# A fused attention, MLP and mixture-of-experts kernel: scores read by half, mask table on GpSimd

## The reference

```python
scores = jnp.einsum('bqhd,bkhd->bhqk', q, k)              # q = layernorm(x), k = v = context, 16 heads of 16
scores = jnp.where(mask == 0, jnp.float32(-1e+20), scores)
attn = jax.nn.softmax(scores / jnp.float32(E ** 0.5), axis=3)
out = jnp.einsum('bhqk,bkhd->bqhd', attn, v).reshape(b, l, e) @ W_out.T + b_out
```

## Time and profile before

| | us |
|---|---|
| median of 3 runs | 1400.29 (1398.33 to 1403.54) |
| the profiled execution, its own time | 1391.09 |
| its span, first to last instruction | 1389.3 |
| attention, first instruction to the next stage's first | 393.8 |
| busy in the span: PE, VectorE, ScalarE, GpSimd | 1225.5, 908.9, 628.3, 576.5 |
| mean granted clock of TensorE | 0.966 |

### The profile page before, as it was taken

One profiled execution on the slowest core, in us unless ns is written; L12 is line 12 of the kernel. 1 busy time (PEld: TensorE's weight loads), 2 busy tenths in 40 slices (PEclk: granted clock), 3 DMA queues, 4 the chain that ended last, 5 costly groups with the idle time before them and its releaser, 6 DMA issues. The chain is left out here.

```text
span 1389.3 us, 29923 instructions
## 1 busy us (share of the span) xinstructions
PE 1225.5 (88%) x10852; PEld 940.3 (68%) x10852; DVE 908.9 (65%) x2674; ACT 628.3 (45%) x1081; POOL 576.5 (41%) x604
## 2 busy tenths in 40 slices
PE   3699999999847798997579999897999999999996
PEld 1355555555423366886467988776999998999995
DVE  7898898898869773225456577444666566665663
ACT  2577777777555571334216633222333333333331
POOL 6899999999900000003200004661333333333333
PEclk9999999999959999999898999999999999999999
DMA  6344344245220001110329205326888877888781
GB/s 225 98 147 138 95 147 141 94 144 190 100 91 0 1 1 46 45 30 1 100 84 255 58 1 183 112 89 214 262 249 250 262 242 248 250 250 257 244 244 65
DMA packets 104193, 196.40 MB, mean 141 GB/s; under 512 B 15632, under 2 KB 86928, under 8 KB 91552
## 3 DMA queue, kind: packets, MB, share of 16 engines
q1 hardware_dynamic: 89792, 178.21, 39.9%
q0 software_dynamic: 14304, 16.93, 5.7%
HBM read 144.70 MB, written 52.23 MB: 142 GB/s over the span
## 5 line engine op out<-in xcount | busy, mean ns | idle before, releaser
L1992 PE MATMUL banks<-moe_w,moe_hT 128*128 128x256 f16 x2640 | 300.6, 273 | 7.2 <-issue 7.1
L1992 PEld LDWEIGHTS banks<-moe_w,moe_hT 128*128 128x128 f16 x2640 | 258.8, 98 | 40.5 <-issue 9.9
L1903 ACT ACTIVATE moe_hf<-banks,moe_b 128x256 f32<-128x256 f32 x440 | 184.9, 472 | 182.7 <-PE banks L1979 148.7
L1847 POOL DMA_INDIRECT out_x<-moe_y,slot_owner x78 | 122.0, 1565 | 285.4 <-DVE moe_y L2225 255.9
L1979 PE MATMUL banks<-moe_rT,moe_w 128*128 128x256 f16 x1872 | 211.8, 273 | 0.0
L745 DVE CUSTOM_DVE_ANT_0 masked<-banks,mask_bias 128x256 f32<-128x256 f32 x512 | 185.8, 418 | 22.6 <-PE banks L515 21.9
L1979 PEld LDWEIGHTS banks<-moe_rT,moe_w 128*128 128x128 f16 x1872 | 183.8, 98 | 21.3
L405 ACT ACTIVATE probsT<-banks 128x1024 f32<-128x1024 f32 x128 | 131.3, 1026 | 64.2 <-PE banks L541 64.1
L2112 DVE TENSOR_TENSOR moe_hT<-moe_hf,moe_hT 128x512 f16<-128x512 f32 x220 | 153.6, 698 | 7.6
L2110 DVE CAST moe_hT<-moe_hf 128x512 f16<-128x512 f32 x220 | 95.2, 433 | 64.1 <-ACT moe_hf L1903 43.9
L1833 POOL DMA_INDIRECT slots_x<-moe_xn,pos x64 | 65.0, 1015 | 153.4 <-DVE pos L2176 123.3
(11 more groups left out here) (323 smaller groups left out, 2006.7 us busy)
## 6 DMA issues: line engine op xcount, KB each, us to landing
moe_w<-moe_halves SPq DMA_DIRECT2D x80, 1024.0 KB, 5.0
moe_halves<-w_cut SPq DMA_DIRECT2D x18, 1024.0 KB, 8.6
slots_x<-empty_row SPq DMA_DIRECT2D x1, 10140.0 KB, 48.8
moe_rows<-slots_x SPq DMA_DIRECT2D x39, 260.0 KB, 5.8
w_in<-in_L_ffn_Wfc SPq DMA_DIRECT2D x8, 1024.0 KB, 6.3
w_in<-in_L_ffn_Wproj SPq DMA_DIRECT2D x8, 1024.0 KB, 6.5
moe_b<-in_L_ffn_bproj SPq DMA_DIRECT2D x39, 128.0 KB
ctx_rows<-in_ctx SPq DMA_DIRECT2D x16, 256.0 KB, 2.8
```

The source lines that it names most:

```text
L1847: pool.indirect_dma_start(out=out_rows, out_offset=bass.IndirectOffsetOnAxis(ap=owner[:, s, t:t + 1], axis=0), in_=y[s % 2][:, t, :], in_o ...
L1903: ins = act.activation(hf[p][:, j, :], src, ACT.Gelu_apprx_tanh, bias=b1[buffer][:, j:j + 1], scale=1.0 / WSCALE)
L1992: ins = pe.matmul(OUT[p][:, t * D:(t + 1) * D], hT[p][:, x, j, t * P:(t + 1) * P], w2[buffer][:, w, j, :], start=(j == 0 and (w, x) == PAR ...
```

## The change

The changed kernel differs in five things.

1. Scores by half. `scores` now issues one matmul: head j of the pair, rows t. PE makes the two scores matmuls of one head and the two transposed ones of the other head (`both_scores(B, hp, 0)`), then a part of the side work, then the other halves (`both_scores(B, hp, 1)`) and the mask. `take_max` reads one half and counts in `s_red` for each, so a half of `psum_s` is free as soon as it has been read.
2. The side work has another order. `fill` 0 goes through `psum_o` and is copied by VectorE, 1 and 2 by ScalarE, 3 by VectorE; the two calls of `project` and `add` are one each; ScalarE's copies stand ahead of the exponent of their head pair.
3. GpSimd makes the mask table (`set_all`), one batch ahead, at the end of its phase behind `split_k`; for batches 0 and 1 before the loop and at the end of its first phase. VectorE waits for `s_ma`.
4. The cutting of the experts' weights (`load_half`, `store_half`, `cut_piece`, now functions of their own with buffers that live through three stages): 9 halves beside attention, two pieces in each phase; 2 beside the MLP, two pieces ahead of its first reduction over partitions, six behind it; 7 in the autocorrelation, ahead of its bias adds. The stores are waited for at the end of the autocorrelation.
5. `mixT` of the autocorrelation lies in the memory of `zf`, and `see_weights` stands behind the first half of the head pair.

```diff
+def load_half(sp, d, w, n):
+    src = expert_half(d, n)
+    if n >= 2:
+        sp.wait_ge(w["cut"], 3 * PIECES * (n - 1))
+    sp.dma_start(w["rows"][n % 2][:].rearrange("p (k f) -> p k f", k=src.shape[1]), src).then_inc(w["in"][n % 2], 16)
+def store_half(sp, w, halves_dram, n):
+    sp.wait_ge(w["cut"], 3 * PIECES * (n + 1))
...
+def cut_piece(pool, w, q):
+    n, i = q // PIECES, q % PIECES
...
+    if i == 0:
+        pool.wait_ge(w["in"][n % 2], 16 * (n // 2 + 1))
+    if i == 0 and n >= 2:
+        pool.wait_ge(w["stored"][n % 2], 16 * (n // 2))
+    pool.tensor_scalar(rows[:, cols], rows[:, cols], WSCALE, None, ALU.mult).then_inc(w["cut"], 1)
...
             for b in range(NB):
                 if b >= 2:
                     load_ctx(b)
                     load_mask(b)
-                load_half(b)
-                if b >= 2:
-                    store_half(b - 2)
+                if b < 2:
+                    load_half(sp, d, w, b)
+                elif b % 2 and (b + 1) // 2 < CUT_BESIDE_ATTENTION:
+                    load_half(sp, d, w, (b + 1) // 2)
+                    store_half(sp, w, halves_dram, (b + 1) // 2 - 2)
...
+            def set_all(b):
+                s = b % 2
+                pool.wait_ge(s_mask[s], 16 * (b // 2 + 1))
+                if b >= 2:
+                    pool.wait_ge(s_mb, b - 1)
+                pool.tensor_scalar(mask_all[s][:], mask_int[s][:], 0, MASKED, ALU.is_equal, ALU.mult).then_inc(s_ma, 1)
+
+            split_k(0)
+            set_all(0)
             for B in PHASES:
-                if real(B + 2):
-                    split_k(B + 2)
                 if B >= -1:
-                    cut(B + 1, 0, PIECES // 2)
+                    cut_piece(pool, g.cut, 2 * (B + 1))
                 if real(B + 2):
                     split_q(B + 2)
...
                 if real(B + 2):
                     add_bias(B + 2)
                 if B >= -1:
-                    cut(B + 1, PIECES // 2, PIECES)
+                    cut_piece(pool, g.cut, 2 * (B + 1) + 1)
+                if real(B + 3):
+                    split_k(B + 3)
+                    set_all(B + 3)
...
+            def both_scores(B, hp, j):
+                for i in range(NQ):
+                    if real(B + 1):
+                        scores(B + 1, hp, j, i)
+                    if real(B):
+                        scoresT(B, hp, 1 - j, i)
...
             for B in PHASES:
                 for hp in range(HP):
+                    both_scores(B, hp, 0)
+                    if hp == 0 and real(B + 2):
...
+                        fill(B + 2, 0)
+                    if hp == 1 and real(B - 1):
...
+                        weigh(B - 1, 3)
+                    if hp == 2 and real(B + 1):
...
                         mask_back(B + 1)
...
+                    if hp == 6 and real(B - 1):
...
+                        project(B - 1)
...
+                    both_scores(B, hp, 1)
+                    if real(B):
+                        scoresT_mask(B, hp)
+                    if hp == 0 and real(B):
+                        pe.wait_ge(s_r, 2 * B + 1)
+                        max_back(B, 1)
...
+            see_mask(0)
+            norm_end(0)
             for B in PHASES:
                 for hp in range(HP):
                     if hp == 0 and real(B):
                         split_max(B, 1)
...
+                    if real(B + 1):
+                        take_max(B + 1, hp, 0)
+                    if hp == 0 and real(B + 2):
+                        fill(B + 2, 0)
+                    if hp == 1 and real(B + 2):
+                        set_live(B + 2)
...
+                    if hp == 5 and real(B + 3) and B == -2:
+                        see_mask(B + 3)
+                    if hp == 0 and real(B + 2) and B >= 0:
+                        see_mask(B + 2)
+                    if hp == 6 and real(B + 2):
+                        fill(B + 2, 3)
                     if hp == 6 and real(B - 1):
-                        add(B - 1, 0)
...
+                        add(B - 1)
+                    if B == NB and hp == 0:
+                        see_weights()
...
                     if real(B + 1):
-                        take_max(B + 1, hp)
-                    if B == -2 and hp == 6:
+                        take_max(B + 1, hp, 1)
+                    if hp == 1 and real(B + 2):
+                        set_mask(B + 2)
+                    if B == -2 and hp == 5:
                         v.wait_ge(s_x[1], 16)
                         measure(*GROUPS[1])
                         norm_begin(1)
...
+            for q in range(AHEAD):
+                cut_piece(pool, g.cut, first + q)
             pool.wait_ge(m_pm, 1)
             pool.partition_all_reduce(all_max[:], part_max[:], P, bass.bass_isa.ReduceOp.max).then_inc(m_am, 1)
+            pool.wait_ge(m_am, 1)
+            for q in range(AHEAD, PIECES * CUT_BESIDE_MLP):
+                cut_piece(pool, g.cut, first + q)
...
+            for b in range(NB):
+                load(b, b % 2)
+                if b in (5, 7, 9, 11, 14):
+                    load_half(sp, d, g.cut, n + 2)
+                    store_half(sp, g.cut, halves_dram, n)
+                    n += 1
...
+            for q in range(PIECES * (CUT_BESIDE_ATTENTION + CUT_BESIDE_MLP), 2 * PIECES * (d["L1_ffn_Wfc"].shape[0] + 1)):
+                cut_piece(pool, g.cut, q)
             pool.wait_ge(c_wr, 4)
```

More of the change, by code:

```diff
@@ L520, in scoresT @@
-            def scoresT(b, hp):
+                if n >= 1 and t == 0:
+                    pe.wait_ge(s_red, 2 * (n - 1) + j + 1)
+                rows = slice(SPLIT * j, SPLIT * j + TERMS)
+                at = j * 512 + t * S
+                ins = pe.matmul(psum_s[:, at:at + S], qT[b % 2][rows, hp, t * P:(t + 1) * P], kT[b % 3][rows, hp, :],
+                                start=(t == 0), stop=(t == NQ - 1))
+                if t == NQ - 1:
+                    ins.then_inc(s_S, 1)
+            def scoresT(b, hp, j, k):
@@ L957, in _ @@
             sp.dma_start(lag["dc"][:], d["dc"]).then_inc(lag["in"], 16)
+            for n in range(CUT_BESIDE_ATTENTION + 1, CUT_BESIDE_ATTENTION + CUT_BESIDE_MLP + 1):
+                load_half(sp, d, g.cut, n)
+                store_half(sp, g.cut, halves_dram, n - 2)
         @block.gpsimd
@@ L1362, in load @@
                 sp.dma_start(ctx_in[s][:], rows[:, b, :, :]).then_inc(c_ctx[s], 16)
-            for b in range(2):
-                load(b, b)
-            with sp.Fori(1, NB // 2) as i:
-                for s in range(2):
-                    load(2 * i + s, s)
+            n, halves = CUT_BESIDE_ATTENTION + CUT_BESIDE_MLP, 2 * (d["L1_ffn_Wfc"].shape[0] + 1)
+            load_half(sp, d, g.cut, n + 1)
+            store_half(sp, g.cut, halves_dram, n - 1)
+            for b in range(NB):
[4 more added lines that the diff above has]
+                    n += 1
+            assert n == halves - 2
+            for n in range(halves - 2, halves):
+                store_half(sp, g.cut, halves_dram, n)
+            for s in range(2):
+                sp.wait_ge(g.cut["stored"][s], 16 * (halves // 2))
             sp.wait_ge(c_lw, 2)
```

315 lines of the change are left out of this document (131 added, 184 removed).

## The result

The changed kernel takes **1409.6 us** in the median of 15 runs (1406.1 to 1419.3), the kernel before 1398.2 us beside it (15 runs, 1395.1 to 1405.4): 1.0087 times as long, with a 95% interval of 1.007 to 1.0104. It is slower by 0.9%, 11.4 us.

A forecast was written before the change was run, and what follows sets the result against it. The prediction took PE's own work, about 19.7 us of a 20.93 us batch, as the bound. Its terms, 4 + 9 - 5 + 2 = +10 us on the median 1400.3, gave 1410 us, range 1391 to 1424.

The forecast's parts named there:

- Start, +9: Program start: first scores wait for GpSimd's first tables, 30.1 us against 18.14; +11.1, 2 given back, +9 us (7 to 12).
- Batch, +4: Attention batches: extra changes of matmul kind and new waits outweigh removed waits, +0.3 us a batch, +4 us over thirteen.
- The table costs nothing here: Attention batches: GpSimd's mask table, taken as 1.5 us, delays nobody, since what waits for GpSimd has several us of lead.
- Rival (d): MLP and attention: small VectorE steps wait for whole GpSimd passes, 8 us more in the MLP, 1418 us; chance 0.08.
- (a): Attention batches gain: waits vanish and extra changes of kind are free, -1.1 us a batch, 1392 us; chance 0.17.
- (b): Head pairs 0 to 2: VectorE becomes the bound, +1 us a batch instead of +0.3, 1419 us; chance 0.18.
- (c): Start's cost and batch's gain cancel: batch -0.4, end of attention -7, 1399 us, no change; chance 0.22.
- End of attention, -5: Attention's tail: last weighing waits for exponents alone, normalisation 4 us earlier, fewer adds, shorter matmuls: -5 us (-3 to -8).
- MLP, +2: MLP and autocorrelation: ten of some 20 small linked VectorE steps meet GpSimd passes, +2 us (0 to 6).
- two before the reduction [...] fit: MLP: two cutting pieces of 3.3 us each fit where GpSimd waited 10.27 us for the reduction over partitions.
- Autocorrelation, nothing: Autocorrelation: context loads behind weights halves on SyncE cost nothing, 5 us at most if one comes late.
- They end some 20 us ahead: Autocorrelation: GpSimd's twenty-eight pieces, 92 to 95 us, end some 20 us ahead of its first bias add.

The follow-up runs named there:

- run 1: The changed kernel, with VectorE again making the mask tables of batches 0 and 1: 1.0039 times the kernel before.
- run 3: The changed kernel, with one cutting piece a batch moved on GpSimd from behind the mask table to ahead of it: batch 20.50 us, 1.0012 times the kernel before.
- run 7: Changed kernel with one piece, not two, ahead of the MLP's first partition reduction, then also transfers held back: reduction starts 11.66, then 6.75 us behind the piece.
- run 8: Changed kernel plus run 1, run 3, MLP pieces behind the reduction, first context loads earlier; second kernel also loads weights halves later: 0.9926, 0.9928 of the kernel before.
- run 5: The changed kernel with no cutting in the MLP stage, its eight pieces moved to the end of the autocorrelation's: 1.0144 times the kernel before.
- 4: The changed kernel with both halves of a head pair's scores issued together, side work behind them: batch 21.80 us, 1.0139 times the kernel before.
- 9: The second kernel of run 8, with score halves issued together in head pairs 3, 5, 7 and exponents ahead of ScalarE's copies there: 0.9925 times the kernel before.

## Why the prediction was right, and where it was not

The forecast was 1410 us and slower, the median is 1409.6. That it came so near is partly luck. Its start was 1400.3, the median of three runs, where fifteen give 1398.2; from there the change is +11.4 and not +10. On the traces' own footing the sum should have been +10 and was +19.2: attention +9.7, MLP +7.2, autocorrelation +2.5. The traced execution of the kernel before was a quick one, 7 below its median, and the MLP of the changed one a slow one, 2.7 above its second profile; neither was known. How much of the +7.2 and the +2.5 is that quick execution stays open. The attention terms are firmer: in six profiles with the same attention stage it takes 403.0 to 403.9 us.

*Start, +9.* Right in place, cause and size: VectorE idle before the reduction of mask 1, released by GpSimd; 8.0 us by the third batch, and 9.0 less at the end of attention without it (run 1). The first scores came at 31.8 instead of 30.1: the table took 1.94 us where I took 1.5, the bias add was 0.5 later, and one linked step (0.80 us) met a subtraction. The page GPSIMD Engine Reference, 4.1 Engine selection, of the Trainium skill, by which a one-input pass runs roughly at line rate (an estimated 0.6 us), does not hold for this one: three times as long. More was made up behind it, too: from 12.6 at the first maximum to 8.0, where I had 2.

*Batch, +4.* The size was right (+0.35 a batch, +0.3 predicted; over the thirteen batches, from first scores to first scores, +5.2 us) and the composition wrong. PE's work rose to 20.3 or 20.5 and not 20.6, for a change of kind costs 0.09 us and not 0.12. The waits are 0.87 and not 0.6, and what I computed them from, the length of VectorE's chain, is not their cause: undisturbed, the chain leaves 0.16 (run 3). The step that failed is "What waits for it has several us of lead. The table costs nothing here". I asked of GpSimd's work only who waits for its results. Nobody does; but moving the table shifted a subtraction by 1.94 us, onto a VectorE step that PE waits for, and that cost 0.85 us a batch, twelve batches in a row.

*Rival (d)*, given a chance of 0.08, had the mechanism, and at the wrong place and in the wrong form: not ten small steps in the MLP that each meet a pass by chance, but one step in attention that meets the same one each time. The rows for it stood in the earlier trace rows: 231 to 1232 ns for one form, and 1153 for the subtraction. I had read the spread as noise to be averaged. The Trainium skill (SBUF — State Buffer, Who interferes with whom) says that a tensor_scalar of VectorE can, in a two-port mode, take the port pair that it shares with GpSimd, and that whoever issues first keeps it for the whole instruction; the trace agrees: the subtraction issued 0.15 us earlier and the step ended 0.06 us behind it. By the same section a one-input pass of GpSimd would hold it as well. For a copy or a cast the trace agrees (0.64 us, ending 0.06 behind the CAST, run 3), for the table it does not: 0.21 us in the middle of its 1.94.

*Rivals (a), (b), (c).* The batch did not gain, though with GpSimd's order mended it would have, by half of what (a) asked for (20.50 against 21.00). (b) named the place, the chain at the batch's beginning; its size, +1 a batch, was not reached. (c) had the batch shorter by 0.4 and the end at -7; neither came.

*End of attention, -5.* It gave 3.5: the lag is 8.0 + 5.2 = 13.2 at the last batch's first scores (354.86 against 341.67) and 9.7 at the end. The last weighing lost its wait as predicted (1.13 us behind the exponents). The normalisation behind it was to come 4 us earlier, on the ground that see_weights would stand where it stood; it stands behind the add of both tiles, which is later (387.30); it came 10.4 us later than before, so only 2.8 of the 4 were gained.

*MLP, +2.* +4.5 to +7.2. The linked steps cost 1.2 up to the part maximum, as supposed. What failed is "two before the reduction [...] fit": by their durations they do, 4.4 us ahead, and the reduction was late all the same (run 7). Up to the first hidden values the stage lost 2.4 to 3.5 us by this and the linked steps together.

The rest of the MLP's loss, 2.1 to 3.7 us, lies behind them, and there TensorE's clock is a rival that I left out. Both traces enter the stage at 1.2 GHz (granted clock 0.50). In the kernel before it rose to 2.4 GHz at 409.7, after TensorE had worked from 406.74 to 409.59 on the second weights and `sw_diag`, fell at 413.2, when TensorE had been busy for 0.62 of the 3.6 us since, and rose again at 416.5; in the changed kernel it stayed at 1.2 GHz until 432.2. Of the stage's first 32 us, 19.3 were at the low clock before, 28.7 and 27.9 in the two profiles after; the first turning of inputs took 0.62 us before and 1.03 after. But the stage doesn't follow the clock alone: the two kernels of run 8 have 20.5 us of it each, and the stage takes 137.8 and 139.7 us. How much the clock costs here, and how much of it is due to the change, isn't shown.

*Autocorrelation, nothing, "5 at most if one comes late".* +2.5 (+4.1 in the second profile): the first context rows behind a megabyte of weights, and then one or two waits in the loop. The bound was right, the value not: 13.5 us a half against 11.3 us for two batches of the loop, 5.64 each in the kernel before, is arithmetic that I didn't do. "They end some 20 us ahead" was wrong as well: the pieces took 106 us from the stage's start, not 92 to 95, and ended 5.9 us ahead, not before 630 but at 654; run 5 showed what two halves more cost there.

## What to carry to other kernels

When work is moved to an engine that isn't the bound, ask of each of its instructions not only who waits for its result but what it will lie beside: on this chip a GpSimd subtraction of 1.16 us held a VectorE step of 0.2 us for 1.1, and in this periodic schedule it did so in twelve batches in a row. A spread such as 231 to 1232 ns in one form can be such a meeting, and the order of the other engine's program is a free variable that removes it. And what comes first in a stage or in the program (a table, a reduction, a queue's first loads) is not covered by the steady state: here three firsts cost 8.0, 2.4 to 3.5 and 1.7 us.

## What the runs showed of the hardware that I had not expected

- A VectorE TENSOR_SCALAR of 128x16 takes 0.21 us beside GpSimd's TENSOR_SCALAR passes (1.94 us, int32 to bf16; 1.50 us, f32) and 1.07 us when GpSimd's subtraction began 0.15 us before it. A CAST or a COPY of GpSimd (0.61 us) holds it as well: 0.64 and 0.42 us, each ending 0.06 behind them.
- GpSimd's compare-and-multiply from int32 to bf16, 128x512, takes 1.94 us; VectorE's takes 0.41.
- The change from tensor work to the partition reduction took GpSimd at most 6.75 us with no transfers and 6.9 to 11.7 beside some 4.3 MB of them (from memsets, 10.4 us beside the same transfers were enough); the change back took 7.0 to 7.7 us.
- A change between kinds of matmul costs TensorE 0.07 to 0.09 us (an estimate from the work of a batch in runs 3, 4, 8 and 9), also where nothing is waited for.
